# A decoder layer in float32: five products of the last two batches' tails from split operands, and new step orders

## The chip, the cores and the metric

The kernel runs on one core of a Trainium2 chip (trn2). The metric is the time on the device in microseconds (us), the median of several executions; lower is better. The profile is of one execution; its span runs from the first to the last thing recorded on the core.

The engines are TensorE (PE; its weight loads are listed as PEld), VectorE (DVE), ScalarE (ACT), GpSimd (POOL) and SyncE (SP), which only issues transfers here. Each works through its own list of instructions in order, and they meet through semaphores.

## The reference

`x` is 4 batches of 256 tokens by 256 channels, `ctx` the same shape. Cut to what is computed:

```python
x = x + attn(layernorm(x), Wqkv, Wo)         # 16 heads of 16, rope, causal
x = x + xattn(layernorm(x), ctx, mask)       # below
x = x + ffn(layernorm(x), ...)               # 8 experts of 176, best 2, and a shared one of 352

def xattn(h, m, mask):
    scores = einsum('bsd,bmd->bsm', h, m) / sqrt(D)
    scores = where(mask, scores, -1e30)
    return softmax(scores) @ m               # zero for a batch without a valid token
```

All of it is float32, and the results have to be near float32 in accuracy.

## The kernel before

**Steps and orders.** Everything is cut into numbered steps, and a table `ORDER` lists for each engine the order of its steps, written out by hand or by a search outside the kernel. A step of one name on several engines is one piece of work: `s.7` is a product on PE and an exp on ACT. The first number of most steps is the batch; `s` runs over 12 per batch, `m` over 12, `tr` over 8, `qk` over 2, `pv`, `h` over 4.

**Attention of batch b.** `ln1`, `ln1n` (L446), `xt` (transposes, L783; copied by ACT, L434), `qk` and `v` (float32 products, L789), rope on DVE (L639, L642) and POOL (L388), a high part of q and k on ACT (`sh`, L499, L500) and a low part on POOL (L395, L398), which are transposed by `tr` (L938) and copied by ACT and DVE. `m` computes scores (L809, L816) only for the row maxima (DVE, L602); `mt` transposes them (L961), ACT copies them, and SP sends them into q_t by a small transfer (L303), which the first `s` of the batch waits for. `s` computes the scores (L830, L834), ACT takes the exp (L522), casts three of them to a high part (`h`, L529), POOL subtracts to get the low part (`h`, L408), and `pv` (L854) multiplies both with the values. DVE adds up the parts (L665).

**The tail of batch b.** It runs through one bank of PSUM, `ps_tail`. `on` and `ot`: the normalised output is transposed and copied by ACT to `tail_t` (L532); `wo` multiplies it by Wo; DVE adds to the residual (L680). `ln2`, `ln2n`, `t2`: the norm, transposed and copied to `tail_t` (L434). `xs`: times `ctxt_s`, DVE masks and takes the maximum (L691), ACT the exp (L538). `pt`: transposed and copied, scaled by `valid` (L543). `ro`: times `ctx_s`, added on DVE (L701). `ln3`, `ln3n`, `t3`: the norm, transposed, its high part on ACT (L434), its low part on DVE (L709). `lg`, `rk`, `ct`: gate logits, ranks, and the weights of the experts, sent through memory by SP. So a tail has three float32 products, `wo`, `xs` and `ro`, each four products of 128 channels by 256 columns, one after the other at L789. The moments of a norm are taken on DVE (L584), and POOL turns them into scale and shift (L366 to L369).

**The feed-forward part.** 28 times `up` and `dn`, 14 for the first two batches and 14 for the last two. `up.m` multiplies 128 hidden rows by 512 tokens for two weights, from split operands: hi by hi, hi by lo, lo by hi (L776, 12 products of 128x512 in all). ACT applies silu (L562), DVE multiplies (L744) and scales by the experts' weights (L753), ACT casts the high part (`dn`, L568), DVE subtracts for the low part (L758), and `dn.m` adds the product with w3 (L885, 12 products of 128x256). The weights' high parts are cast by ACT (`w12`, `w3`; L468, L477) and their low parts made by POOL (L415, L419), in the place of the raw ones. `up` and `dn` need few engines besides PE and stand between the steps of the last tails.

**Fillers.** `early.n` and `late.n` are n products of zeros (L895) that nobody reads; 16 more run at the start.

The first up step waits for the third norm of batch 1; steps of `up` from 3 on wait for the last exp, since they take over banks; `dn.0` waits for the last rope and values.

## Time and profile before

| | us |
|---|---|
| median of 3 runs | 272.88 (272.65 to 274.71) |
| the profiled execution | 272.15 |
| its span | 270.3 |
| PE busy in the span | 257.3 |
| ACT, DVE, POOL busy | 174.0, 166.3, 119.2 |
| granted clock of PE, mean of the span | 1.00 |

Times in rows are in us unless marked ns. A row of the timeline gives start, duration, engine, line, operation, tiles and count, and in brackets the engine's idle time before it with what ended it. On PE the duration of a product holds a modelled tail that overlaps the next product; the chain of waits shows pieces without it. Counts of the float32 products are twice the calls in the kernel.

### The profile page before, as it was taken

How to read it: one execution, taken by the hardware profiler on the slowest of the kernel's cores; microseconds unless marked ns; L12 is line 12 of the kernel's file. 1: busy time of each engine (PE TensorE's matmuls, PEld its weight loads, DVE VectorE, ACT ScalarE, POOL GpSimd, SP SyncE). 2: the span in 40 equal slices, each digit the busy share in tenths (PEclk: the TensorE clock that was granted, in tenths of full speed). 3: DMA queues.
4: the chain of work that ended last, by engine and by line, in shares of the span. 5: the costliest groups of instructions: out<-in, count | busy, mean ns of one | idle time of the engine just before them, and what ended most of it. 6: DMA issues, size and time to landing. Idle time of an engine off the chain costs nothing.

```text
span 270.3 us, 4890 instructions
## 1 busy us (share of the span) xinstructions
PE 257.3 (95%) x1806; PEld 209.2 (77%) x1806; DVE 166.3 (62%) x361; ACT 174.0 (64%) x290; POOL 119.2 (44%) x133
## 2 busy tenths in 40 slices
PE   7799999999999999959999999999999999999994
PEld 2467666777876888847788988888989898888884
DVE  3388984878778758856452678453755634545463
ACT  7478669979878998979789667536555313223230
POOL 4457915895398897967567453051500000000000
PEclk9999999999999999999999999999999999999999
DMA  7891000000000028000019700000000279000002
GB/s 243 326 397 70 0 2 1 4 2 2 2 0 0 5 79 274 2 5 0 4 49 266 192 1 2 1 0 2 0 0 2 79 168 247 16 0 4 0 0 78
DMA packets 11878, 17.08 MB, mean 63 GB/s; under 512 B 1904, under 2 KB 8272, under 8 KB 11856
## 3 DMA queue, kind: packets, MB, share of 16 engines
q1 hardware_dynamic: 11856, 16.78, 20.1%
q8 instruction: 14, 0.23, 0.4%
q14 instruction: 8, 0.07, 0.1%
HBM read 15.63 MB, written 1.08 MB: 62 GB/s over the span
## 4 chain that ended last, share of the span: by engine, by line
PE 84%; DMA 5%; DVE 4%; ACT 3%; SPq 1%; issue 1%; POOL 1%; DVEq 0%; ACTq 0%
PE bank L776 31%; PE bank L885 14%; PE bank L789 12%; PE bank L938 4%; PE bank L830 4%; DMA res<-x 3%; PE bank L816 3%; PE bank L854 3%; PE bank L783 3%; PE bank L834 3%; PE bank L809 3%; DVE negm L602 2%; PE bank L811 1%; PE bank L818 1%; DMA q_t<-negm_t 1%
## 5 line engine op out<-in xcount | busy, mean ns | idle before, releaser
L408 POOL TENSOR_TENSOR prob_lo<-prob,prob_hi 128x1536 f16<-128x1536 f32 x16 | 49.9, 3121 | 17.4 <-ACT prob_hi L529 17.4
L776 PE MATMUL bank<-x_hi,w_hi 128*128 128x512 f32 x112 | 45.5, 407 | 0.0
L776 PE MATMUL bank<-x_hi,w_lo 128*128 128x512 f32 x112 | 44.2, 395 | 0.0
L776 PE MATMUL bank<-x_lo,w_hi 128*128 128x512 f32 x112 | 44.1, 393 | 0.0
L602 DVE TENSOR_REDUCE negm<-bank 128x2 f32<-128x512 f32 (+1 forms) x48 | 31.5, 687 | 7.0 <-PE bank L811 4.0
L758 DVE TENSOR_TENSOR h_lo<-h_c,h_hi 128x512 fp32r<-128x512 f32 x28 | 19.9, 714 | 23.5 <-ACT h_hi L568 23.4
L744 DVE TENSOR_TENSOR h_c<-bank,h_s 128x512 f32<-128x512 f32 x28 | 19.3, 689 | 24.5 <-PE bank L776 19.8
L562 ACT ACTIVATE h_s<-bank 128x512 f32<-128x512 f32 x28 | 16.7, 598 | 26.2 <-PE bank L776 26.1
L885 PE MATMUL bank<-w_hi,h_hi 128*128 128x256 f32 x112 | 32.8, 293 | 0.1
L568 ACT CAST h_hi<-h_c 128x512 fp32r<-128x512 f32 x28 | 17.2, 616 | 23.5 <-DVE h_c L753 14.0
L885 PE MATMUL bank<-w_lo,h_hi 128*128 128x256 f32 x112 | 31.6, 282 | 0.0
L885 PE MATMUL bank<-w_hi,h_lo 128*128 128x256 f32 x112 | 31.6, 282 | 0.0
L522 ACT ACTIVATE prob<-bank 128x512 f32<-128x512 f32 x48 | 27.5, 597 | 4.5 <-PE bank L834 3.6
L830 PE MATMUL bank<-q_t,k_t 113*128 113x512 f32 (+1 forms) x64 | 23.1, 417 | 2.8 <-DMA q_t<-negm_t 2.8
L776 PEld LDWEIGHTS bank<-x_hi,w_lo 128*128 128x128 f32 x112 | 21.0, 188 | 5.0
L529 ACT CAST prob_hi<-prob 128x1536 f16<-128x1536 f32 x16 | 23.6, 1474 | 1.1 <-PE bank L854 1.0
L776 PEld LDWEIGHTS bank<-x_hi,w_hi 128*128 128x128 f32 x112 | 21.1, 189 | 4.0
L776 PEld LDWEIGHTS bank<-x_lo,w_hi 128*128 128x128 f32 x112 | 21.1, 188 | 4.0
L789 PE MATMUL bank<-wqkv_s,xt_s 128*128 128x512 f32 (+1 forms) x64 | 22.5, 489 | 1.3 <-ACT xt_s L434 1.3
L885 PEld LDWEIGHTS bank<-w_hi,h_hi 128*128 128x128 f32 x112 | 21.3, 190 | 0.8 <-DVE h_lo L758 0.3
L885 PEld LDWEIGHTS bank<-w_lo,h_hi 128*128 128x128 f32 x112 | 21.3, 191 | 0.6
L415 POOL TENSOR_TENSOR w_lo<-w_raw,w_hi 128x512 fp32r<-128x512 f32 x14 | 18.0, 1285 | 7.8 <-ACT w_hi L468 7.8
(128 smaller groups left out, 566.1 us busy)
## 6 DMA issues: line engine op xcount, KB each, us to landing
w_raw<-w SPq DMA_DIRECT2D x3, 1792.0 KB, 8.4
comb_b<-comb_dram SPq DMA_DIRECT2D x8, 256.0 KB, 5.2
res<-x SPq DMA_DIRECT2D x4, 256.0 KB, 6.8
ctxt_s<-ctx_t SPq DMA_DIRECT2D x4, 256.0 KB, 7.6
ctx_s<-ctx SPq DMA_DIRECT2D x4, 256.0 KB, 7.1
out<-res SPq DMA_DIRECT2D x8, 128.0 KB, 1.8
comb_b<-comb_dram SPq DMA_DIRECT2D x4, 224.0 KB, 5.1
wqkv_s<-wqkv SPq DMA_DIRECT2D x1, 768.0 KB, 4.6
```

Of the source, the lines that this page charges most:

```text
L408: eng.tensor_tensor(prob_lo[:, b % 2], prob[:, b % 2], prob_hi[:, b % 2], ALU.subtract)\
L415: eng.tensor_tensor(lo, raw, hi.bitcast(F32), ALU.subtract).then_inc(s[w + "_ok"], 1)
L522: act.activation(prob[:, g % 2, i, :], ps_s[b % 2][:], ACT.Exp, scale=DH ** -0.5)\
L529: act.copy(prob_hi[:, b % 2], prob[:, b % 2]).then_inc(s["p_hi"], 1)
L568: act.copy(h_hi[:, m % 2], h_c[:, m % 2]).then_inc(s["hhi_ok"], 1)
L602: dve.tensor_reduce(maxes, bk[:].rearrange("p (r k) -> p r k", r=maxes.shape[-1]), AX.X, ALU.max, negate=True).then_inc(s["sm_max"], 1)
L744: ins = dve.tensor_tensor(h_c[:, m % 2], h2_bank[h_pair(m)][:], h_s[:, m % 2], ALU.mult)
L758: dve.tensor_tensor(h_lo[:, m % 2], h_c[:, m % 2], h_hi[:, m % 2].bitcast(F32), ALU.subtract)\
L776: ins = pe.matmul(dst, a(k), c(k), start=(k == 0 and i == 0), stop=(k == kt - 1 and i == 2))
L789: ins = pe.matmul(dst, lhs(k), rhs(k), start=(k == 0), stop=(k == KC - 1))
L830: pe.matmul(ps_s[n % 2][:, c * w:(c + 1) * w], k_t[0:SHIFT + 1, b % 2, j, k0:k0 + P], q_t[0:SHIFT + 1, b % 2, j, :, k0:S], start=(c == 0), ...
L885: ins = pe.matmul(y_tile(t), a[:, m % 2, tok], c[:, j, :], start=(j == 0 and i == 0 and t % 2 == 0), stop=(j == FT - 1 and i == 2), skip_g ...
```

## The change

`SPLIT` names five of the twelve products of the tails: xs and ro of batch 2, and wo, xs and ro of batch 3. For these the ACT copy of `ps_tail` writes `tail_hi` in the reduced format instead of `tail_t`; a new DVE step `lo` writes `tail_lo`, the copy's remainder; a new step `sd` makes the high part of Wo, ctx_t or ctx on ACT and the low part on POOL, in the place of the raw data; and PE computes hi by hi, hi by lo and lo by hi instead of one float32 product. The new tiles lie partly where attention's tiles are, so `t2.2` and `sd.0` on ACT wait for the last `pv`. The orders of all engines are new. Cut to the code and to the pieces of the orders that are spoken of below:

```diff
...
+SPLIT = (("xs", 2), ("ro", 2), ("wo", 3), ("xs", 3), ("ro", 3))
...
 ORDER = {
     "SP": """
-        ln1.0 mt.0 mt.1 mt.2 ct.0 ro.0 w3.0 mt.3 ct.1 cb.0 ro.1 y.0 ct.2 ct.3 cb.1 y.1
+        ln1.0 mt.0 mt.1 mt.2 ro.0 mt.3 w3.0 ro.1 ct.0 ct.1 cb.0 ct.2 ct.3 cb.1 y.0 y.1
     """,
     "POOL": """
-        ln1.0 ln1.1 qk.0 sh.0 qk.1 qk.2 sh.1 w12.0 ln1.2 ln1.3 qk.3 w12.1 sh.2 tr.7 sh.3 h.0 qk.4 h.1 sh.4 h.2 h.3
-        qk.5 sh.5 w12.2 ln2.0 w12.3 h.4 h.5 qk.6 sh.6 ln3.0 h.6 qk.7 h.7 sh.7 w12.4 w12.5 h.8 ln2.1 w12.6 h.9 h.10
-        w3.0 w3.1 w12.7 ln3.1 h.11 w12.8 w3.2 h.12 h.13 w3.3 w12.9 ln2.2 h.14 w3.4 w3.5 w3.6 h.15 w12.10 w3.7 ln3.2
-        w12.11 w3.8 w3.9 w3.10 ln2.3 w3.11 w12.12 w3.12 w3.13 w12.13 ln3.3
+        ln1.0 ln1.1 qk.0 ln1.2 sh.0 qk.1 qk.2 sh.1 w12.0 tr.7 w12.1 sh.2 qk.3 sh.3 qk.4 h.0 qk.5 h.1 sh.4 sh.5 h.2
+        h.3 ln1.3 w12.2 h.4 ln2.0 h.5 w12.3 qk.6 w12.4 sh.6 ln3.0 h.6 qk.7 h.7 sh.7 w12.5 h.8 ln2.1 w12.6 h.9 w12.7
+        h.10 h.11 ln3.1 h.12 w12.8 h.13 w3.0 w12.9 h.14 ln2.2 h.15 w3.1 sd.0 w3.2 sd.1 w3.3 w3.4 w12.10 ln3.2 w3.5
+        w12.11 sd.2 w3.6 sd.3 w12.12 w3.7 w3.8 w3.9 ln2.3 w3.10 w12.13 sd.4 ln3.3 w3.11 w3.12 w3.13
...
     "ACT": """
-        ln1n.0 xt.0 ln1n.1 w12.0 sh.0 xt.1 w12.1 v.0 vm.0 tr.0 tr.1 sh.1 v.1 w12.2 tr.4 tr.5 ln1n.2 w12.3 w12.4 sh.2
...
-        h.10 w12.8 s.33 xs.1 w3.0 pt.1 w3.1 s.34 w3.2 s.35 w3.3 mt.3 h.11 w3.4 vm.3 s.36 ln3n.1 s.37 s.38 t3.1 s.39
-        s.40 h.12 lg.1 s.41 up.0 h.13 ct.1 dn.0 up.1 ot.2 s.42 s.43 s.44 w12.9 dn.1 s.45 s.46 h.14 ln2n.2 s.47 up.2
...
+        ln1n.0 xt.0 ln1n.1 v.0 sh.0 xt.1 vm.0 ln1n.2 tr.0 tr.1 sh.1 w12.0 sh.2 w12.1 tr.4 tr.5 xt.2 v.1 sh.3 mt.0
+        vm.1 tr.8 tr.9 s.0 tr.12 s.1 s.2 tr.13 h.0 s.3 s.4 sh.4 s.5 h.1 s.6 sh.5 s.7 s.8 s.9 h.2 s.10 w12.2 s.11
...
+        s.33 w12.7 s.34 xs.1 s.35 pt.1 mt.3 h.11 w12.8 vm.3 s.36 s.37 s.38 h.12 ln3n.1 s.39 s.40 t3.1 s.41 s.42 h.13
+        s.43 lg.1 w12.9 s.44 w3.0 up.0 ct.1 h.14 ot.2 up.1 s.45 dn.0 w3.1 s.46 s.47 h.15 w12.10 up.2 w3.2 ln2n.2
+        dn.1 w12.11 w3.3 dn.2 up.3 sd.0 t2.2 up.4 sd.1 xs.2 dn.3 w3.4 pt.2 up.5 w3.5 w3.6 w3.7 sd.2 up.6 dn.4 ln3n.2
+        t3.2 w12.12 dn.5 lg.2 up.7 up.8 w3.8 sd.3 dn.6 ct.2 w3.9 ot.3 up.9 dn.7 w12.13 ln2n.3 w3.10 up.10 w3.11 dn.8
+        t2.3 sd.4 xs.3 dn.9 dn.10 pt.3 up.11 dn.11 up.12 ln3n.3 w3.12 dn.12 w3.13 t3.3 up.13 dn.13 lg.3 up.14 dn.14
...
     "DVE": """
-        ln1.0 ln1.1 qk.0 ln1.2 qk.1 ln1.3 v.0 qk.2 vm.0 kt.2 kt.3 v.1 qk.3 m.0 m.1 kt.6 m.2 kt.7 m.3 m.4 m.5 m.6 m.7
-        m.8 m.9 m.10 m.11 zero.0 zero.1 kt.10 kt.11 vm.1 qk.4 kt.14 kt.15 m.12 m.13 pv.0 m.14 m.15 m.16 m.17 m.18
...
+        ln1.0 ln1.1 zero.0 zero.1 qk.0 ln1.2 v.0 qk.1 vm.0 qk.2 kt.2 kt.3 qk.3 m.0 m.1 kt.6 m.2 kt.7 m.3 m.4 m.5 m.6
+        m.7 m.8 m.9 m.10 m.11 v.1 vm.1 kt.10 kt.11 qk.4 kt.14 ln1.3 kt.15 qk.5 m.12 m.13 m.14 m.15 m.16 m.17 pv.0
...
+        up.2 pv.14 dn.1 up.3 lo.0 dn.2 xs.2 up.4 pv.15 xc.2 dn.3 lo.1 up.5 ro.2 ln3.2 dn.4 up.6 t3.2 on.3 lg.2 dn.5
+        rk.2 up.7 dn.6 lo.2 up.8 wo.3 ln2.3 dn.7 up.9 dn.8 lo.3 up.10 xs.3 dn.9 xc.3 lo.4 dn.10 ro.3 ln3.3 up.11
...
     "PE": """
-        xt.0 qk.0 qk.1 v.0 xt.1 qk.2 tr.0 tr.1 v.1 tr.2 tr.3 qk.3 tr.4 m.0 tr.5 m.1 tr.6 m.2 tr.7 m.3 xt.2
-        early.1 m.4 m.5 m.6 m.7 m.8 m.9 m.10 m.11 early.3 mt.0 tr.8 tr.9 v.2 tr.10 s.0 tr.11 s.1 tr.12 s.2 tr.13
-        qk.4 s.3 s.4 tr.14 early.3 tr.15 s.5 s.6 m.12 m.13 pv.0 s.7 m.14 m.15 s.8 m.16 s.9 m.17 s.10 m.18 m.19
...
-        m.45 pt.1 m.46 m.47 ro.1 mt.3 pv.9 s.36 s.37 pv.10 s.38 late.1 t3.1 s.39 s.40 pv.11 lg.1 s.41 up.0 s.42
-        s.43 ct.1 late.1 up.1 ot.2 pv.12 wo.2 s.44 pv.13 s.45 s.46 dn.0 s.47 up.2 t2.2 up.3 pv.14 xs.2 up.4 pt.2
-        pv.15 dn.1 ro.2 dn.2 up.5 dn.3 t3.2 up.6 lg.2 dn.4 up.7 ct.2 up.8 ot.3 dn.5 wo.3 dn.6 dn.7 up.9 t2.3
-        up.10 xs.3 up.11 pt.3 dn.8 ro.3 dn.9 dn.10 up.12 t3.3 up.13 dn.11 lg.3 dn.12 dn.13 up.14 ct.3 up.15
...
+        xt.0 qk.0 v.0 qk.1 xt.1 qk.2 tr.0 tr.1 v.1 tr.2 tr.3 qk.3 tr.4 m.0 tr.5 m.1 tr.6 m.2 tr.7 xt.2 m.3
+        early.1 m.4 m.5 m.6 m.7 m.8 m.9 m.10 m.11 early.3 mt.0 tr.8 tr.9 qk.4 tr.10 s.0 tr.11 tr.12 s.1 s.2
+        tr.13 tr.14 qk.5 tr.15 s.3 s.4 m.12 s.5 m.13 s.6 m.14 m.15 m.16 s.7 m.17 pv.0 m.18 m.19 s.8 s.9 m.20
+        s.10 m.21 m.22 s.11 m.23 pv.1 mt.1 tr.16 tr.17 early.2 pv.2 s.12 s.13 tr.18 tr.19 s.14 pv.3 tr.20 tr.21
+        v.2 early.1 ot.0 s.15 tr.22 wo.0 s.16 s.17 tr.23 pv.4 xt.3 s.18 m.24 s.19 m.25 m.26 t2.0 m.27 m.28 xs.0
+        m.29 m.30 qk.6 pt.0 m.31 s.20 ro.0 s.21 m.32 m.33 s.22 qk.7 m.34 m.35 s.23 pv.5 mt.2 t3.0 tr.24 tr.25
+        pv.6 lg.0 tr.26 s.24 s.25 tr.27 v.3 tr.28 pv.7 tr.29 ct.0 tr.30 s.26 s.27 tr.31 ot.1 s.28 m.36 wo.1 s.29
+        s.30 m.37 s.31 m.38 pv.8 m.39 m.40 s.32 m.41 s.33 m.42 t2.1 m.43 m.44 xs.1 m.45 s.34 m.46 s.35 pv.9 m.47
+        pt.1 late.1 mt.3 ro.1 pv.10 s.36 s.37 late.1 s.38 s.39 late.1 s.40 pv.11 late.5 t3.1 s.41 s.42 pv.12
+        s.43 lg.1 s.44 up.0 pv.13 ct.1 s.45 s.46 ot.2 up.1 wo.2 s.47 pv.14 dn.0 up.2 up.3 t2.2 pv.15 up.4 xs.2
+        dn.1 dn.2 pt.2 up.5 ro.2 up.6 up.7 t3.2 dn.3 lg.2 dn.4 up.8 ct.2 dn.5 ot.3 dn.6 wo.3 up.9 up.10 t2.3
+        up.11 xs.3 dn.7 dn.8 pt.3 dn.9 ro.3 dn.10 up.12 up.13 t3.3 dn.11 dn.12 lg.3 up.14 dn.13 up.15 ct.3 up.16
...
-        wo_s = sb("wo_s", [P, KC, C])
-        ctx_s = sb("ctx_s", [P, 2, NT, C])
-        ctxt_s = sb("ctxt_s", [P, 2, KC, S])
+        wo_s, wo_lo = raw_and_lo(sb, "wo", [P, KC, C])
+        ctx_s, ctx_lo = raw_and_lo(sb, "ctx", [P, 2, NT, C])
+        ctxt_s, ctxt_lo = raw_and_lo(sb, "ctxt", [P, 2, KC, S])
...
+        tail_hi = sb("tail_hi", [P, KC, S], F32R)
+        tail_lo = sb("tail_lo", [P, KC, S], F32R)
+        wo_hi = sb("wo_hi", [P, KC, C], F32R)
+        ctx_hi = sb("ctx_hi", [P, 2, NT, C], F32R)
+        ctxt_hi = sb("ctxt_hi", [P, 2, KC, S], F32R)
...
+        def side(n):
+
+            name, b = SPLIT[n]
+            if name == "wo":
+                return wo_s[:], wo_hi[:], wo_lo[:]
+            return [v[:, b % 2] for v in ((ctxt_s, ctxt_hi, ctxt_lo) if name == "xs" else (ctx_s, ctx_hi, ctx_lo))]
         def halves(a_hi, a_lo, b_hi, b_lo):
...
                         .then_inc(s["w3_ok"], 1)
+                elif part == "sd":
+                    raw, hi, lo = side(b)
+                    eng.wait_ge(s["side_hi_ok"], b + 1)
+                    if SPLIT[b][0] == "wo":
+                        eng.wait_ge(s["wo_ps"], NT * SPLIT[b][1])
+                    eng.tensor_tensor(lo, raw, hi.bitcast(F32), ALU.subtract).then_inc(s["side_ok"], 1)
                 elif part == "ln2":
...
                     act.wait_ge(s["ot_ps"], b + 1)
-                    act.copy(tail_t[:], halves_of(ps_tail)).then_inc(s["oh_ok"], 1)
+                    act.copy((tail_hi if ("wo", b) in SPLIT else tail_t)[:], halves_of(ps_tail)).then_inc(s["oh_ok"], 1)
                 elif part == "t2":
-                    xn_hi_copy(1, b, tail_t[:])
+                    if b == 2:
+                        act.wait_ge(s["o_ps"], NG * B)
+                    xn_hi_copy(1, b, (tail_hi if ("xs", b) in SPLIT else tail_t)[:])
                 elif part == "xs":
...
                     act.wait_ge(s["valid_ok"], 1)
-                    act.activation(tail_t[:], halves_of(ps_tail), ACT.Identity, scale=valid[:, b:b + 1])\
+                    act.activation((tail_hi if ("ro", b) in SPLIT else tail_t)[:], halves_of(ps_tail), ACT.Identity, scale=valid[:, b:b + 1])\
                         .then_inc(s["xph_ok"], 1)
+                elif part == "sd":
+                    name, m = SPLIT[b]
+                    raw, hi, lo = side(b)
+                    if b == 0:
+                        act.wait_ge(s["o_ps"], NG * B)
+                    if name == "wo":
+                        act.wait_ge(s["wo_in"], 16)
+                    else:
+                        act.wait_ge(s[("ctxt_in" if name == "xs" else "ctx_in") + str(m % 2)], 16 * (m // 2 + 1))
+                    act.copy(hi, raw).then_inc(s["side_hi_ok"], 1)
                 elif part == "t3":
...
                         .then_inc(s["on_ok"], 1)
+                elif part == "lo":
+                    name, m = SPLIT[b]
+                    if name == "wo":
+                        dve.wait_ge(s["oh_ok"], m + 1)
+                        dve.tensor_tensor(tail_lo[:], halves_of(ps_tail), tail_hi[:].bitcast(F32), ALU.subtract)\
+                            .then_inc(s["tail_lo_ok"], 1)
+                    elif name == "xs":
+                        dve.wait_ge(s["xn_hi_ok1"], m + 1)
+                        dve.tensor_tensor(tail_lo[:], halves_of(ps_tail), tail_hi[:].bitcast(F32), ALU.subtract)\
+                            .then_inc(s["tail_lo_ok"], 1)
+                    else:
+                        dve.wait_ge(s["xph_ok"], m + 1)
+                        dve.scalar_tensor_tensor(out=tail_lo[:], in0=halves_of(ps_tail), scalar=valid[:, m:m + 1],
+                                                 in1=tail_hi[:].bitcast(F32), op0=ALU.mult, op1=ALU.subtract)\
+                            .then_inc(s["tail_lo_ok"], 1)
                 elif part == "wo":
...
                     whole_product(dst, lambda k: a[:, k, tok], lambda k: w[:, k, :]).then_inc(s[name], 1)
+            def split_rows(n, name):
+
+                raw, hi, lo = side(n)
+                pe.wait_ge(s["side_ok"], n + 1)
+                pe.wait_ge(s["tail_lo_ok"], n + 1)
+                for t, dst in enumerate(out_tiles):
+                    tok = slice(t * P, (t + 1) * P)
+                    split_product(dst, lambda k: tail_hi[:, k, tok], lambda k: tail_lo[:, k, tok],
+                                  lambda k: hi[:, k, :], lambda k: lo[:, k, :]).then_inc(s[name], 1)
+
             def row_maxima_scores(b, f):
...
                     pe.wait_ge(s["wo_in"], 16)
-                    product(tail_t, wo_s, "wo_ps")
+                    if ("wo", b) in SPLIT:
+                        split_rows(SPLIT.index(("wo", b)), "wo_ps")
+                    else:
+                        product(tail_t, wo_s, "wo_ps")
                 elif part == "xs":
...
                     pe.wait_ge(s[f"ctxt_in{b % 2}"], 16 * (b // 2 + 1))
-                    product(tail_t, ctxt_s[:, b % 2], "xs_ps")
+                    if ("xs", b) in SPLIT:
+                        split_rows(SPLIT.index(("xs", b)), "xs_ps")
+                    else:
+                        product(tail_t, ctxt_s[:, b % 2], "xs_ps")
                 elif part == "ro":
...
                     pe.wait_ge(s[f"ctx_in{b % 2}"], 16 * (b // 2 + 1))
-                    product(tail_t, ctx_s[:, b % 2], "ro_ps")
+                    if ("ro", b) in SPLIT:
+                        split_rows(SPLIT.index(("ro", b)), "ro_ps")
+                    else:
+                        product(tail_t, ctx_s[:, b % 2], "ro_ps")
                 elif part == "lg":
...
```

`out_tiles` are the two halves of `ps_tail`; `split_product` is the helper of `up` (L776).

## Rows read from the trace of the kernel before

**Rows 1.** The page's first part: busy us, share of the span, instructions.
```profile
PE 257.3 (95%) x1806; PEld 209.2 (77%) x1806; DVE 166.3 (62%) x361; ACT 174.0 (64%) x290; POOL 119.2 (44%) x133
```

**Rows 2.** Table by stretches: us, then each engine's busy us (instructions), clock, DMA share, GB/s.
```profile
119.00:262.00 143.00, 142.93 (x937) 123.27 (x937) 77.06 (x167) 76.30 (x128) 37.70 (x39) 1.00 0.19 49
46.00:115.00 69.00, 68.12 (x607) 54.64 (x606) 52.57 (x119) 60.30 (x103) 54.91 (x43) 1.00 0.11 36
```

**Rows 3.** Timeline of PE: start, us, engine, line, operation, count, idle before.
```profile
64.49 0.66 PE L938 MATMUL bank<-ident,stk 128*128 128x128 f32 x4 [0.37 <-POOL stk L398]
...
114.90 0.38 PE L961 MATMUL bank<-ident,negm 128*16 128x128 f32 x2
...
118.72 0.51 PE L830 MATMUL bank<-q_t,k_t 113*128 113x512 f32 x1 [2.83 <-DMA q_t<-negm_t]
...
121.02 0.66 PE L783 MATMUL bank<-ident,tail 128*128 128x128 f32 x4
...
124.92 0.58 PE L776 MATMUL bank<-x_hi,w_hi 128*128 128x512 f32 x1
```

**Rows 4.** Chain of waits, in order of time: start us, us, what (instruction count).
```profile
172.45 1.43 PE bank L885 x12
173.88 1.73 PE bank L789 x8
...
178.47 2.78 PE bank L776 x12
```

**Rows 5.** Groups by line and form: count, busy us, mean ns, idle before.
```profile
L408 POOL TENSOR_TENSOR prob_lo<-prob,prob_hi 128x1536 f16<-128x1536 f32 x16 | 49.9, 3121 | 17.4 <-ACT prob_hi L529 17.4
...
L522 ACT ACTIVATE prob<-bank 128x512 f32<-128x512 f32 x48 | 27.5, 597 | 4.5 <-PE bank L834 3.6 <-POOL prob_lo L408 0.6
L529 ACT CAST prob_hi<-prob 128x1536 f16<-128x1536 f32 x16 | 23.6, 1474 | 1.1 <-PE bank L854 1.0
...
L415 POOL TENSOR_TENSOR w_lo<-w_raw,w_hi 128x512 fp32r<-128x512 f32 x14 | 18.0, 1285 | 7.8 <-ACT w_hi L468 7.8
...
L753 DVE TENSOR_TENSOR h_c<-h_c,comb_b 128x512 f32<-128x512 f32 x22 | 15.8, 717 | 2.6 <-DVE h_c L744 0.5
...
L468 ACT CAST w_hi<-w_raw 128x512 fp32r<-128x512 f32 x14 | 8.5, 613 | 0.8 <-DMA w_raw<-w 0.8
...
L616 DVE MEMSET q_t<- 64x2048 f32 x2 | 3.5, 1765 | 0.9 <-issue 0.9
...
L709 DVE TENSOR_TENSOR x_lo<-bank,x_hi 128x512 fp32r<-128x512 f32 x4 | 2.8, 690 | 2.8 <-ACT x_hi L434 2.8
...
L532 ACT COPY tail_t<-bank 128x512 f32<-128x512 f32 x4 | 2.3, 586 | 2.4 <-PE bank L783 2.4
```

**Rows 6.** Timeline of DVE, then of POOL, near 149 us.
```profile
149.59 1.22 DVE L753 TENSOR_TENSOR h_c<-h_c,comb_b 128x512 f32<-128x512 f32 x1
...
147.12 3.14 POOL L408 TENSOR_TENSOR prob_lo<-prob,prob_hi 128x1536 f16<-128x1536 f32 x1 [0.56 <-ACT prob_hi L529]
```

**Rows 7.** Timeline of DVE in the opening.
```profile
11.14 0.69 DVE L639 TENSOR_TENSOR rope_c<-bank,cos_t 128x512 f32<-128x512 f32 x1 [3.03 <-PE bank L789]
...
14.27 0.75 DVE L584 BATCH_NORM_STATS2 stats<-res 128x6 f32<-128x256 f32 x2 [1.78 <-DMA res<-x]
```

**Rows 8.** Timeline of ACT, then of POOL, in the opening.
```profile
14.95 0.58 ACT L434 COPY xt_s<-bank 128x512 f32<-128x512 f32 x1
...
14.57 0.73 POOL L395 TENSOR_TENSOR stk<-rot,stk 128x256 fp32r<-128x256 f32 x1 [0.73 <-ACT stk L499]
```

**Rows 9.** Timeline of DVE, then of POOL: the third norm of batch 1.
```profile
115.10 0.88 DVE L701 SCALAR_TENSOR_TENSOR res<-bank,xs_rec,res 128x256 f32<-128x256 f32 x2 [0.57 <-PE bank L789]
...
118.50 0.23 POOL L369 TENSOR_SCALAR shift<-shift 128x2 f32<-128x2 f32 x1
```

**Rows 10.** Timeline of SP's queue: the issue of w3's load.
```profile
101.10 0.37 SPq L335 DMA_DIRECT2D w_raw<-w  x1
```

**Rows 11.** The page's DMA issues: count, KB each, median us to landing.
```profile
w_raw<-w SPq DMA_DIRECT2D x3, 1792.0 KB, 8.4
```

More of the change, by code:

```diff
@@ L68 @@
-        h.10 w12.8 s.33 xs.1 w3.0 pt.1 w3.1 s.34 w3.2 s.35 w3.3 mt.3 h.11 w3.4 vm.3 s.36 ln3n.1 s.37 s.38 t3.1 s.39
-        s.40 h.12 lg.1 s.41 up.0 h.13 ct.1 dn.0 up.1 ot.2 s.42 s.43 s.44 w12.9 dn.1 s.45 s.46 h.14 ln2n.2 s.47 up.2
-        t2.2 up.3 w3.5 w3.6 w3.7 h.15 xs.2 dn.2 pt.2 dn.3 w12.10 up.4 w12.11 up.5 ln3n.2 dn.4 t3.2 dn.5 up.6 lg.2
-        w12.12 w3.8 w3.9 w3.10 up.7 ct.2 dn.6 up.8 w3.11 ot.3 dn.7 w12.13 ln2n.3 up.9 t2.3 dn.8 up.10 w3.12 xs.3
-        dn.9 pt.3 dn.10 w3.13 up.11 ln3n.3 up.12 dn.11 t3.3 up.13 dn.12 dn.13 lg.3 up.14 dn.14 up.15 up.16 dn.15
@@ new lines @@
+        s.18 t2.0 h.5 xs.0 pt.0 s.19 w12.4 s.20 sh.6 h.6 s.21 s.22 w12.5 ln3n.0 s.23 mt.2 t3.0 h.7 tr.24 tr.25 lg.0
+        sh.7 s.24 s.25 w12.6 tr.28 tr.29 ct.0 s.26 ot.1 h.8 s.27 s.28 s.29 v.3 h.9 s.30 s.31 ln2n.1 s.32 t2.1 h.10
+        s.33 w12.7 s.34 xs.1 s.35 pt.1 mt.3 h.11 w12.8 vm.3 s.36 s.37 s.38 h.12 ln3n.1 s.39 s.40 t3.1 s.41 s.42 h.13
+        s.43 lg.1 w12.9 s.44 w3.0 up.0 ct.1 h.14 ot.2 up.1 s.45 dn.0 w3.1 s.46 s.47 h.15 w12.10 up.2 w3.2 ln2n.2
+        dn.1 w12.11 w3.3 dn.2 up.3 sd.0 t2.2 up.4 sd.1 xs.2 dn.3 w3.4 pt.2 up.5 w3.5 w3.6 w3.7 sd.2 up.6 dn.4 ln3n.2
@@ L103 @@
+        dn.14 dn.15 up.17 dn.16 up.18 dn.17 up.19 dn.18 up.20 dn.19 up.21 dn.20 up.22 dn.21 up.23 dn.22 up.24
+        dn.23 up.25 up.26 up.27 dn.24 dn.25 dn.26 dn.27
     """,
```

33 lines of the change are left out of this document (11 added, 22 removed).

## The prediction

> **What bounds the kernel now.** First the page's line of busy shares: TensorE (PE) is busy for 257.3 of 270.3 us [rows 1]. A share hides where, so the table by stretches comes next. From 119 to 262 us PE is busy for 142.93 of 143 us at a granted clock of 1.00 (2.4 GHz), while DVE and ACT are busy for 77 and 76 us; from 46 to 115 us it is 68.12 of 69 us [rows 2]. Then the timeline of PE, for its idle time: the one long wait is 2.83 us, for the small transfer of the row maxima of batch 3, after mt.3 [rows 3]. So the span is nearly the sum of what PE issues, in the order in which it issues it. Anything taken off PE after 119 us comes off the end, as long as the step it is taken from is still ready when PE reaches it. Last, the chain of waits gives the price of a step as PE sees it (start to start, without the modelled tail that the timeline adds): 1.73 us for a float32 product of a tail, 1.43 us for the twelve 128x256 products of a down step, 2.78 us for an up step [rows 4].
>
> **The change part by part.**
>
> 1. Five float32 products become split ones. A split one is 2 tiles x 2 k x 3 = 12 products of 128x128 by 128x256, exactly the shape, type and number of a down step. 1.73 - 1.43 = 0.30 us each, five times: -1.5 us [rows 4]. All five stand where PE never idles [rows 2]. The down step is so near that I take the row as it is; the bounds are 0 (a split product as long as a float32 one) and -1.5.
> By the Trainium skill (FP8 and Floating Point Precision, TensorE Precision Notes) a true float32 product is four passes over the array, and the split leaves the low-by-low one out. By that count alone the saving would be a quarter of 1.73 us, 0.43 each and 2.2 in all; the down step's row says 0.30, and the row decides.
>
> 2. The halves have to be made. Weight side: five ACT casts of 0.61 us and five POOL subtractions of 1.29 us [rows 5], 3.1 and 6.4 us on engines that have room after 119 us. Behind them queue the casts and low halves of w3 and the norms, none of which PE reaches within a microsecond, so I cost them at nothing; if that cover were gone, one subtraction is 1.29 us. Activation side: five DVE subtractions like that of x_lo, 0.69 us [rows 5], each between the ACT copy of ps_tail and the PE product. Between transpose and product the chain was one ACT operation of 0.59 us and is now that plus 0.69, 1.3 to 1.4 with hand-offs. For xs.2, ro.2 and xs.3 the new order puts an up step (2.78) in between: hidden. For wo.3 only dn.6 (1.43) stands there: 0 to 0.1 us of wait. For ro.3 only dn.9, and ACT has the casts dn.9 and dn.10 ahead of pt.3, about 0.6 more: some 0.5 us. I take +0.5, between 0 and 1.5 (all five late by 0.3).
> A DVE operation with two SBUF operands (h_c by comb_b) that ran beside a POOL subtraction took 1.22 us, where 0.72 is the mean [rows 5, 6]. Five more POOL operations make more such meetings, up to 0.5 us each on DVE; they reach PE only through a chain of the kind just named, which is inside the upper bound.
> The Trainium skill (SBUF — State Buffer, SBUF: two separate sides) says that GpSimd and a DVE operation with two SBUF inputs hold one port pair exclusively, for the whole instruction. The row agrees in kind; the page alone would allow 1.29 us a meeting, 6.4 in all, against 2.5 by the row.
>
> 3. The opening. zero.0 and zero.1 (1.77 us each [rows 5]) move from behind m.11 to before qk.0. DVE has 3.0 us free there, up to 11.14 [rows 7], so 3.5 us with their issue overrun by about 1 us, and rot, sh.0 and the ACT copy xt.1 behind it, which began at 14.95 [rows 8], slip by as much. On POOL sh.0 now stands behind ln1.2, whose x is read at 14.27 [rows 7]; sh.0 began at 14.57 [rows 8] and now begins near 16.8, and tr.0 waits for it. Against that, ACT's w12.0 and w12.1 and DVE's ln1.3 and v.1 leave the stretch. Walked step by step with the durations above, mt.0 comes 0.4 us later. Behind mt.0 DVE no longer has the 3.5 us before kt.10, so qk.4 and qk.5 cover the transfer, and the filler products and the wait before tr.15 go: -1.0. Together -0.6 (bounds +1 and -1.5).
>
> 4. mt.3. PE waits 2.83 us from the end of pv.9 to s.36 [rows 3]. Now ro.1 (1.73) is behind mt.3, beside a pv, so that wait falls to about 1.1. It isn't simply won: the third norm of batch 1 starts from ro.1, and up.0 needs it. From ro.1's sum (115.10) through POOL (done 118.73) [rows 9] and ACT to t3.1 at 121.02 [rows 3] took 6 us, and POOL now has h.11 (3.12 [rows 5]) ahead of ln3.1. Walked from mt.3's start: transfer landed at 3.8 us, s.36 to s.38 paced by exps of 0.6, POOL free of h.11 at 5.3, ln3.1 done 6.8, ACT through h.12 and ln3n.1 at 8.8, t3.1 at 8.9, s.41 to s.44 and lg.1 behind exps, up.0 at 13.3. In these 13.3 us stand 9.2 us of products (mt.3, ro.1, three pv, nine s steps, t3.1, lg.1): 4.1 lost. Before, mt.3 to up.0 was 114.90 to 124.92 [rows 3], with 6.3 us of products (three pv, six s steps): 3.7 lost. That is +0.4, less 0.2 for the filler behind ct.1 that goes. The new order itself puts five filler products before t3.1. I take 0 (bounds -2, the transfer's wait won, and +4, rival C).
>
> 5. SP. The load of w3 was issued at 101.10 [rows 10] and lands in 8.4 us [rows 11]; it now goes behind mt.3's transfer, so it lands near 122. ACT reads it first in w3.0, behind s.44, and PE in dn.0, both after 125: nothing, with some 3 us of cover. ct.0 behind ro.1 is waited for by ct.1 alone, and y.0's stores behind cb.1 are not the last: nothing.
>
> 6. The middle, 46 to 115 us, is reordered throughout. Priced by steps its work is about 62 us of 69, so some 6 us are small gaps and fillers. The fillers of the two PE orders are 14 before and 15 after, besides the 16 of the warm-up, so no large stall seems to have gone. One has: sh.4, sh.5 and qk.5 now stand ahead of batch 0's last prob_lo on POOL, and the wait of 0.37 us for stk [rows 3] goes. I take -0.4, between -2 and +2 (the same POOL work delays pv.3, and ot.0 behind it, by up to 2 us).
>
> Sum: -1.5 + 0.5 - 0.6 + 0 + 0 - 0.4 = -2.0 us. The profiled execution took 272.15 us around its span of 270.3, and lies 0.73 below the median of the runs, 272.88. So 268.3 for the span, 270.15 for such an execution, and 270.9 for the median.
>
> **The rivals.**
>
> A. The order gains too: the 1.7 us of the transfer's wait that ro.1 covers stay won, because ACT is ahead of my walk, and the middle loses 1 us less of its 6: 270.9 - 1.7 - 1.0 = 268.2. For it: some 8 us of PE are lost before 125 us, more than item 1 could give. Against it: the number of fillers.
>
> B. The splits' gain is eaten: the five lo chains cost 1.5 us, their upper bound, and the opening's +0.4 stands without the -1.0: 272.88 - 1.5 + 1.5 + 0.4 = 273.3. For it: 0.69 us more in each of five chains. Against it: after 119 us PE waited for no tail before [rows 2].
>
> C. Slower: ACT paces the last attention batch with no up step to cover it. Before, up.0 came after s.41, now after s.44 and pv.12. Three more exps (0.60) and one more prob_hi cast (1.47) lie ahead of it, 3.3 us of ACT, and a prob_lo of 3.12 us on POOL before pv.12 [rows 5]. It decides if ACT comes to s.36 later than 3.8 us after mt.3 (my walk has it there at 3.4), since from there each step of item 4 hangs on an ACT step. Then 3.3 us of ACT, and half of POOL's 3.12 (lg.1 overlaps the rest), come on top for 1.7 us of products bought, and nothing of the opening's gain is left: 272.88 - 1.5 + 0.5 + 3.3 + 1.6 - 1.1 = 275.7.
>
> **How the numbers follow.** The forecast's own case (269.9 to 272.2) has a chance of 0.42, A 0.31, B 0.17, C 0.10. One per cent, about what a measurement of this kernel can tell from no change, is 2.73 us: faster is below 270.15, slower above 275.6. A lies below it but for its upper part, and the lower edge of the forecast's case does too: faster 0.33. C gives 0.09 slower; the rest, 0.58, is within 1%. The range leaves out the lower part of A, and C: 268.0 to 273.8.
>
> **What would show it.** The chain of waits should have pieces of twelve products in 1.43 us for five of the twelve products of the tails. The waits of PE should show no wait for the transfer above 1.5 us, and waits of 0.1 to 0.5 us on tail_lo before wo.3 and ro.3. PE should be busy for all but 1 us from up.0 to the last down steps. up.0 should begin near 126 us, and from there to the end should be about 142.6 us (145.4 before, less 1.5 for the splits and 1.8 for three s steps and a pv already done, plus 0.5). Item 1 is wrong if a split product takes 1.6 us or more; item 2 if PE's waits for tail_lo add up to over 1 us (B); item 4 if up.0 begins before 124 (A) or after 129 (C).

## The result, and the profile after

| us | before | after |
|---|---|---|
| median of 20 runs each, side by side | 272.71 (271.03 to 274.71) | 274.81 (273.08 to 277.95) |
| ratio after to before | | 1.0084, 95% interval 1.0063 to 1.0106 |
| profiled execution, its span | 272.15, 270.3 | 273.39, 271.9 |
| mt.0, up.0 start in it | 34.39, 124.92 | 35.30, 128.85 |
| from up.0 to the end | 145.4 | 143.05 |

The change makes the kernel 0.8% slower; 270.9 was forecast, and 273.8 was the upper end of the range. The mean granted clock of an execution lies between 0.98 and 1.00 for each kernel here, so beside the ratios, which leave out executions over 1.5% above the fastest of their kernel, stand spans "at full clock", the means over the executions at 0.998 or above (44 of 119 of before, mean 269.8; 6 of 20 of after, 271.8). At full clock the change costs 2.0 us.

The page's line for PE and the table by stretches of after (columns as in [rows 1, 2]):
```profile
PE 257.9 (95%) x1822; PEld 208.0 (76%) x1827; DVE 173.6 (64%) x366; ACT 175.8 (65%) x295; POOL 128.7 (47%) x138
...
46.00:115.00 69.00, 67.34 (x622) 53.47 (x624) 51.25 (x115) 59.91 (x103) 53.95 (x44) 1.00 0.03 10
119.00:129.00 10.00, 8.90 (x92) 6.07 (x92) 5.55 (x17) 8.61 (x13) 8.62 (x8) 1.00 0.69 230
129.00:262.00 133.00, 132.57 (x836) 115.59 (x836) 78.66 (x160) 71.99 (x125) 40.63 (x43) 1.00 0.17 49
```
PE's busy time didn't fall at all, though 1.5 us of products went: filler products and the modelled tails count as busy, and hide short waits. PE's idle time moved: 1.66 us in 46 to 115 us, where before had 0.88, and 1.10 in 119 to 129 us, where before had none:
```profile
119.00:129.00 10.00, 10.00 (x99) 7.63 (x98) 5.18 (x19) 9.19 (x14) 7.87 (x4) 1.00 0.00 0
```
That row is before's. ACT is busy there for 9.2 of the 10 us too, more than the 8.6 of after, but PE has up.0 to do from 124.92 on. In after PE has, up to 128.85, only steps that hang on ACT and POOL.

PE's timeline at the steps of [rows 3], then the waits of PE (in total, times, longest):
```profile
115.78 0.39 PE L1018 MATMUL bank<-ident,negm 128*16 128x128 f32 x2 [0.35 <-DVE negm L634]
...
124.01 0.66 PE L830 MATMUL bank<-ident,tail 128*128 128x128 f32 x4 [0.25 <-ACT tail L466]
...
128.85 0.58 PE L823 MATMUL bank<-x_hi,w_hi 128*128 128x512 f32 x1
```
```profile
PE bank L836 <- ACT xt_s L454: 2.4, 2, 1.7
...
PE bank L911 <- POOL prob_lo L422: 0.8, 2, 0.6
...
PE bank L823 <- DVE tail_lo L721: 0.3, 1, 0.3
```
The wait for the transfer, 2.83 us in [rows 3], is gone. mt.3 to up.0 takes 13.07 us (the walk said 13.3). What is left of single waits is small, but for xt_s in the opening: 1.7 us.

To place losses I subtract from a step's start the work that PE issued ahead of it, priced by [rows 4] and like rows (up 2.78, down 1.43, float32 product 1.73, split 1.43, s and m steps 0.36 to 0.44, fillers nothing). Of this "lost time", in before and after: at mt.0 14.6 and 15.5; at mt.1 18.5 and 19.6; at ot.0 20.0 and 22.05; at mt.3 25.8 and 27.8; at up.0 29.9 and 32.1; at up.17 31.3 and 34.1. Three places: the opening (+0.9), mt.1 to ot.0 (+1.0), and the last part, where 1.5 us of products went and 0.5 more is lost than before. With 0.2 at each of two other places that is 2.8 lost and 1.5 gained; 0.3 more behind up.27 makes the 1.6 by which the two spans differ.

### The profile page after: what moved, and what is told of

The parts are those of the page before. It is cut to its first block, busy times and chain, and to the rows that moved or that the text cites. A ratio compares the mean times of both kernels' runs of the same rounds, so it can differ in the third digit from the quotient of the medians.

```text
span 271.9 us, 4950 instructions
## 1 busy us (share of the span) xinstructions
PE 257.9 (95%) x1822; PEld 208.0 (76%) x1827; DVE 173.6 (64%) x366; ACT 175.8 (65%) x295; POOL 128.7 (47%) x138
## 4 chain that ended last, share of the span: by engine, by line
PE 78%; POOL 7%; DVE 5%; issue 3%; ACT 3%; DMA 1%; SPq 1%; DVEq 0%; ACTq 0%; POOLq 0%
PE bank L823 32%; PE bank L942 13%; PE bank L836 8%; PE bank L995 5%; PE bank L887 4%; POOL prob_lo L422 3%; PE bank L911 3%; PE bank L873 3%; PE bank L866 2%; PE bank L891 2%; DVE negm L634 2%; PE bank L830 2%; DMA res<-x 1%; POOL rot L402 1%; PE bank L868 1%
## 5 line engine op out<-in xcount | busy, mean ns | idle before, releaser
L823 PE MATMUL bank<-x_hi,w_hi 128*128 128x512 f32 x112 | 44.9, 401 | 0.0
L634 DVE TENSOR_REDUCE negm<-bank 128x2 f32<-128x512 f32 (+1 forms) x48 | 31.9, 686 | 7.2 <-PE bank L868 4.6
L805 DVE TENSOR_TENSOR h_lo<-h_c,h_hi 128x512 fp32r<-128x512 f32 x28 | 22.7, 812 | 19.7 <-ACT h_hi L600 19.4
L942 PEld LDWEIGHTS bank<-w_hi,h_lo 128*128 128x128 f32 x112 | 21.4, 191 | 0.0
```

The lines of the kernel that those rows point to most:

```text
L634: dve.tensor_reduce(maxes, bk[:].rearrange("p (r k) -> p r k", r=maxes.shape[-1]), AX.X, ALU.max, negate=True).then_inc(s["sm_max"], 1)
L805: dve.tensor_tensor(h_lo[:, m % 2], h_c[:, m % 2], h_hi[:, m % 2].bitcast(F32), ALU.subtract)\
L823: ins = pe.matmul(dst, a(k), c(k), start=(k == 0 and i == 0), stop=(k == kt - 1 and i == 2))
L942: ins = pe.matmul(y_tile(t), a[:, m % 2, tok], c[:, j, :], start=(j == 0 and i == 0 and t % 2 == 0), stop=(j == FT - 1 and i == 2), skip_g ...
```

## The experiments

### Orders and splits apart

Before's orders with the three splits of batch 3, and after's orders without any split:
```diff
-SPLIT = (("xs", 2), ("ro", 2), ("wo", 3), ("xs", 3), ("ro", 3))
+SPLIT = (("wo", 3), ("xs", 3), ("ro", 3))       # and every order of before, with sd, lo put in
+SPLIT = ()                                      # the other: after's orders without sd, lo
```


> The orders of before, with only the three splits of batch 3 (wo, xs, ro) and their sd and lo steps put in by hand. Theory 1 (the splits pay, the new orders cost): each split takes 0.30 us off TensorE (1.43 for 1.73), the chain of a lo step gives back some 0.2 to 0.5 at wo.3 and ro.3, so 0.3 to 0.9 us faster than before, span near 269.7. Theory 2 (the splits themselves cost, through the halves to be made on ACT, POOL and DVE): 0.5 to 2 us slower than before, with waits for tail_lo and for low halves of w3 and h.

> The orders of after without the five splits: the sd and lo steps are left out and all twelve products of the tails are float32. Theory 1: the orders cost 2.8 us before up.0 (TensorE idle summed in the trace: 29.9 us lost before up.0 in before, 32.1 in after, and 0.9 of it before mt.0) and little behind, so 2.0 to 3.0 us slower than before and about 1 us slower than after. Theory 2: the orders are neutral, within 0.5 us of before, and faster than after.


Measured: 1.0006 (0.9975 to 1.0037) for the splits, 270.2 at full clock; 1.0073 (1.0039 to 1.0108) for the orders, 272.2. So at full clock the orders cost 2.4 us, the five splits in them give 0.5 back (by the ratios, 1.0084 with them and 1.0073 without, nothing), and three splits in the old order give nothing. The orders are the fault, and most or all of the splits' gain is eaten.

Table by stretches of the orders alone: from 119 to 129 us PE has the gaps of after, and then, in this execution, its clock is granted at half (1.2 GHz) under up.0, which took 4.1 us (2.97 in after, where the clock stayed at 1.00).
```profile
119.00:129.00 10.00, 8.90 (x89) 6.04 (x90) 5.31 (x16) 8.54 (x13) 8.54 (x8) 0.97 0.70 233
129.00:131.00 2.00, 2.00 (x6) 1.56 (x6) 1.57 (x9) 1.66 (x5) 2.00 (x1) 0.50 0.00 0
```

### The opening

Four tries: after with the memsets back behind m.11 and sh.0 ahead of ln1.2 (e3); every engine in before's order up to mt.0, after's behind it (e5); and, in the order of before, the memsets in front alone (e9), and ln1.2 in front alone (e10). Last, after with sh.0 back alone (e16).
```diff
 "DVE", e9:   -... m.11 zero.0 zero.1 kt.10        +ln1.0 ln1.1 zero.0 zero.1 qk.0
 "POOL", e10: -ln1.1 qk.0 sh.0 qk.1 qk.2 sh.1 w12.0 ln1.2    +ln1.1 qk.0 ln1.2 sh.0 qk.1
 "POOL", e16: -ln1.1 qk.0 ln1.2 sh.0               +ln1.1 qk.0 sh.0 ln1.2
```


> After, with two moves of the opening undone: zero.0 and zero.1 on DVE back behind m.11, and on POOL sh.0 ahead of ln1.2. Theory 1 (the opening is a part of the loss): xt.1's copy on ACT starts near 15 us in place of 16.0, mt.0 near 34.4 in place of 35.3, and the end comes 0.5 to 0.9 us earlier than in after; theory 1b: the idle time of 1.74 us before qk.2 is also what lowers the granted clock to 0.99 in most runs of after, so with it gone the clock of the runs is 1.00 and the median falls by a further 1 us. Theory 2 (the later steps absorb it): mt.0 is earlier but mt.1 (56.7 in after) is not, and the time is that of after within 0.3 us.

> All five splits. Every engine works in the order of before up to its step mt.0 (on DVE up to m.11), and in the order of after behind it; the memsets zero.0 and zero.1 are thus back behind m.11, with v.1 ahead of them. Theory 1 (what the orders lose is lost in three places: 0.9 us before mt.0, 1.0 between mt.1 and ot.0, 0.2 at mt.3 to up.0): mt.0 near 34.5 us in place of 35.3, and the span 0.9 shorter than after's undisturbed one of 271.7, near 270.9, ratio to before near 1.004. Theory 2 (the early memsets paid: with them behind m.11 the copies before tr.10 and tr.14 come later and PE loses before mt.1 what it gained before mt.0): mt.0 near 34.5 but mt.1 not earlier than 56.7, span 271.5 to 272.5, ratio near 1.007.

> The kernel before with one part of the new orders alone: DVE's memsets zero.0 and zero.1 stand ahead of qk.0 and no longer behind m.11. No splits. Theory 1 (the memsets in front push the first rope step on DVE, and rot, the stk copies and tr.0 behind it; that is the opening's loss of 0.9 us): mt.0 starts 0.6 to 1.0 us later than in before (34.4), and what the freed 3.5 us behind m.11 give back before mt.1 is under 0.5: span 0.3 to 0.8 longer. Theory 2 (as the prediction had it: +0.4 before mt.0 and -1.0 behind it): mt.0 near 34.8, mt.1 at 56.8 or earlier, span 0.6 shorter.

> The kernel before with another part alone: POOL's ln1.2 stands ahead of sh.0, as in the new orders, and not behind w12.0. No splits. Theory 1 (POOL waits for the moments of the third x tile before it makes the rows that tr.0 needs, so that tr.0 and all behind it come later): sh.0 on POOL near 16.5 us in place of 14.57, tr.0 and mt.0 later by 0.5 to 1.5 us, span as much longer. Theory 2 (PE has qk.2 to do meanwhile and is not hurt): mt.0 within 0.2 us of before, span the same.

> After with one step moved back: POOL's sh.0 ahead of ln1.2. Theory 1 (PE's tr.0 waits for sh.0, and sh.0 for the third x tile's moments through ln1.2): sh.0 about 15.5 us in place of 16.57, mt.0 0.5 us earlier than 35.4 and the span 0.3 to 0.6 shorter than 271.7. Theory 2 (in the new order the early memsets on DVE alone set the pace): mt.0 and the span within 0.2 of after's.


Measured: e3 1.0211 (mt.0 at 34.82, but v.1 stands behind the memsets there and PE waits 3.0 us for q_t after mt.0; not a clean undo). e5 1.0046 (1.0018 to 1.0073), 271.4 at full clock: mt.0 at 34.79, but mt.1 at 56.99 and not before after's 56.71, as its theory 2 had it. Behind mt.0 PE then waits 0.9 us for DVE's k_t, a wait that after doesn't have, so undoing the opening gives back 0.4 us and not all that it costs. e9 1.0057 (1.0024 to 1.0090). e10 1.0024 (0.9997 to 1.0051), mt.0 at 34.67, 270.6 at full clock. e16 1.0096 (1.0062 to 1.0130), no gain. The profiled execution of e9 took 278.55 us, 4.7 above the median of its twelve, so from it I take how the steps follow on each other, and not a price.

The reason shows when DVE's timelines stand together: second x tile's moments, memsets, first rope step. After, then the memsets alone (e9), then an execution with the memsets where they were (e13, below):
```profile
6.77 0.75 DVE L616 BATCH_NORM_STATS2 stats<-res 128x6 f32<-128x256 f32 x2 [2.03 <-DMA res<-x]
...
10.41 1.76 DVE L648 MEMSET q_t<- 64x2048 f32 x1 [0.48 <-issue]
12.21 0.69 DVE L671 TENSOR_TENSOR rope_c<-bank,cos_t 128x512 f32<-128x512 f32 x1
```
```profile
8.71 0.76 DVE L584 BATCH_NORM_STATS2 stats<-res 128x6 f32<-128x256 f32 x2 [4.09 <-DMA res<-x]
...
12.37 1.76 DVE L616 MEMSET q_t<- 64x2048 f32 x1 [0.48 <-issue]
14.16 0.69 DVE L639 TENSOR_TENSOR rope_c<-bank,cos_t 128x512 f32<-128x512 f32 x1
```
```profile
8.64 0.75 DVE L616 BATCH_NORM_STATS2 stats<-res 128x6 f32<-128x256 f32 x2 [3.95 <-DMA res<-x]
...
11.07 0.69 DVE L671 TENSOR_TENSOR rope_c<-bank,cos_t 128x512 f32<-128x512 f32 x1 [1.39 <-PE bank L836]
```
The moments of the second tile began between 6.7 and 8.7 us, whatever the kernel, as its transfer landed (in twenty profiles, twelve times by 7.1 and four times behind 8.6). With the memsets behind m.11 the rope starts at 10.96 to 11.22 us in all twelve such profiles: the idle time of [rows 7] was slack for the transfer. With the memsets in front it starts 5.45 us after the moments, in all eight: 12.2 at best, 14.2 at worst. PE pays in full (after, then e9):
```profile
16.63 1.98 PE L836 MATMUL bank<-wqkv_s,xt_s 128*128 128x512 f32 x4 [1.74 <-ACT xt_s L454]
```
```profile
18.57 2.48 PE L789 MATMUL bank<-wqkv_s,xt_s 128*128 128x512 f32 x4 [3.80 <-ACT xt_s L434]
```
In e9 the clock is then granted at 0.71 to 0.73 from 19 to 25 us, and mt.0 comes at 38.4. e16, the other late landing with the memsets in front, has mt.0 at 37.9 without a fall of the clock. With the memsets behind m.11 a late landing costs little: mt.0 at 34.8 (e5) and 35.3 (e13), where landings by 7.1 us have 33.8 to 34.7. So the 0.9 us between the two profiled executions of before and after is the price of an early landing.

### The middle

After with sh.5 moved behind h.3 on POOL (e4), on POOL and ACT (e15); before's orders up to ot.0, after's behind (e6); and in the order of before the cluster of qk.5 alone (e17).
```diff
 "PE", e17:   -tr.14 early.3 tr.15 ... m.23 qk.5 mt.1     +tr.14 qk.5 tr.15 ... m.23 mt.1
 "POOL", e17: -qk.4 h.1 sh.4 h.2 h.3 qk.5 sh.5            +qk.4 qk.5 h.1 sh.4 sh.5 h.2 h.3
 "ACT", e17:  -s.7 sh.4 s.8 ... s.13 sh.5                 +sh.4 s.7 sh.5 s.8
```


> After, with sh.5 on POOL moved from before h.2 to behind h.3, so that prob_lo of groups 2 and 3 start 1.5 us earlier. Theory 1 (POOL's order delays pv.3, on.0 and ot.0, which start at 62.4 and 66.0 in after): ot.0 0.8 to 1.5 us earlier, TensorE's lost time before ot.0 down by about as much, unless tr.20 waits for sh.5 instead; 0.3 to 1 us faster than after. Theory 2 (another engine sets that stretch): tr.20 waits as long as pv.3 is earlier, no change within 0.3 us.

> All five splits. Every engine works in the order of before up to ot.0 (DVE up to on.0, ACT up to ot.0, POOL up to sh.5), and in the order of after behind it. Theory 1 (two microseconds of the orders' loss lie before ot.0, and the splits are worth what after showed of them, 0.4 to 1.0): ot.0 near 63.5 us in place of 66.0, less work ahead of it; span 269.5 to 270.2 in an undisturbed execution, ratio to before 0.998 to 1.001. Theory 2 (the loss is a debt of the order as a whole: what is won before ot.0 is lost again before mt.2, since the chain of batch 1 is what paces there): span 271 or more, ratio above 1.004.

> After with sh.5 moved back on both engines that make it: on ACT behind s.13, on POOL behind h.3, as in before. Theory 1 (ACT's casts for sh.5, 1.2 us, and POOL's 1.5 us stand ahead of h.2 and h.3, the low halves that pv.2 and pv.3 wait for; together they make ot.0 late): ot.0 starts 0.8 to 1.2 us earlier than 66.0, and of it 0.5 to 1.0 stays to the end, span 270.7 to 271.2. Theory 2 (ot.0 is late because the row maxima and the exps as a whole come later, and sh.5 is only shifted): ot.0 within 0.3 of 66.0, span 271.7 or more.

> The kernel before with one cluster of the new orders alone: qk.5 on PE behind tr.14, in the place of three filler products, on DVE ahead of m.12, on POOL ahead of h.1, and sh.5 on ACT and POOL ahead of h.2. No splits. Theory 1 (the rope and the rows of qk.5 stand ahead of the row maxima, casts and low halves that batch 0's values wait for; the work is only shifted on PE, the delay of pv.1 to pv.3 is not): ot.0 0.5 to 1.0 us later than in before relative to mt.0 (29.1 us after it), up.0 likewise, span 270.2 to 270.8 against 269.7. Theory 2 (the cluster fills what was filler and wait, and the loss is elsewhere): span 269.7 or less.


Measured: e4 1.0120 (1.0074 to 1.0166), ot.0 at 66.61, no gain: mt.0 to ot.0 takes 31.1 us, in after 30.7. e15 1.0138 (1.0086 to 1.0189), ot.0 at 68.51, worse: 31.9 us from mt.0, which was itself 1.3 late. e6 1.0100 (1.0066 to 1.0135): ot.0 at 63.28, and 2.3 us of wait for ACT's q_t right behind it, where the two orders meet. e17 1.0082 (1.0053 to 1.0112), 272.3 at full clock (three executions): the cluster alone costs 2.5 us. From mt.0 to ot.0 it loses 8.4 us, before 5.4. Of the rest, ot.0 to mt.3 and up.0 to the end repeat before's within 0.1 us. Waits of PE in e17, 34 to 70 us:
```profile
PE bank L853 <- issue: 0.9, 1, 0.9
PE bank L853 <- POOL prob_lo L407: 0.9, 1, 0.9
PE bank L960 <- DVE negm L601: 0.8, 1, 0.8
```
The rope and rows of qk.5 (DVE, ACT and POOL) stand ahead of the maxima and low halves that mt.1 and the values wait for. Undoing one link inside the new order doesn't help, since the other steps were placed for it.

### From mt.3 to up.0

In the order of before: ro.1 behind mt.3 alone (e11); s.42, s.43, pv.12, s.44 ahead of up.0 (e18).
```diff
 "PE", e11: -m.47 ro.1 mt.3 pv.9                          +m.47 mt.3 ro.1 pv.9
 "PE", e18: -s.41 up.0 s.42 s.43 ct.1 late.1 up.1 ot.2 pv.12 wo.2 s.44
            +s.41 s.42 s.43 pv.12 s.44 up.0 ct.1 ot.2 late.1 up.1 wo.2
```


> The kernel before with a third part alone: on PE ro.1 stands behind mt.3 and not ahead of it, so that its 1.73 us lie in the wait for the small transfer of the row maxima. No splits. Theory 1 (the wait becomes shorter but the third norm of batch 1, which starts from ro.1, comes 2 us later and up.0 with it, so nothing is won): mt.3 1.7 us earlier, t3.1 and up.0 at the same time as before within 0.5, span the same within 0.3. Theory 2 (the transfer's wait is real idle time, and its cover is a gain): up.0 1.0 to 1.7 us earlier, span 269 or less.

> The kernel before with the last cluster alone: s.42, s.43, pv.12 and s.44 ahead of up.0 on PE and ACT, and the transposes ot.2 ahead of up.1. No splits. Theory 1 (without an up step between them these steps are paced by ACT's exps of 0.60 us and its casts of 1.47, so PE idles where before it had up.0 to do): up.0 starts 2.5 to 3.5 us later for 1.7 us of products, span 0.8 to 1.5 longer, 270.5 to 271.2; fewer executions at full clock. Theory 2 (nothing is lost, since what ACT has done ahead of up.0 it need not do behind it): span within 0.3 of 269.7.


Measured: e11 1.0050 (1.0018 to 1.0082), 271.0 at full clock, 1.2 more than before. mt.3 is 0.4 us earlier and not 1.7, as theory 1 had it; it waits for the last maxima (PE's timeline of e11):
```profile
114.51 0.39 PE L960 MATMUL bank<-ident,negm 128*16 128x128 f32 x2 [1.32 <-DVE negm L601]
114.73 1.46 PE L788 MATMUL bank<-ctx_s,tail_t 128*128 128x256 f32 x6
```
ro.1 had filled that wait. e18 1.0192 (1.0165 to 1.0219): up.0 at 130.95, and the clock granted at 0.50 to 0.84 from 120 to 136 us. None of its 6 executions was at full clock, but beside them only 1 of before's 11 was. Of its cost, 2.2 us are a wait of pv.12 for DVE's on.2, which is the edit's own; it shows the danger of the place, not the price in after.

### What eats the splits' gain

Before's orders up to pv.15, four splits behind (e7); after with ACT's pt.3 ahead of dn.10 (e8); after with ACT's sd.3, w3.8, w3.9 behind ot.3 (e14); then, from the three splits in before's order, the sums of batch 3 moved to another bank and the wait for tail_lo put off, both at once (e12), and up.10 moved on DVE too (e13).
```diff
 e12: def rows_bank(b): return ps_out if b == 3 else ps_tail     # the sums leave the bank of the transposes
-                pe.wait_ge(s["tail_lo_ok"], n + 1)
                 for t, dst in enumerate(out_tiles(SPLIT[n][1])):
                     for k in range(KC):      # tail_hi by hi, tail_hi by lo
...
+                    if t == 0:
+                        pe.wait_ge(s["tail_lo_ok"], n + 1)
                     for k in range(KC):      # tail_lo by hi
 e13, "DVE": -xs.3 dn.9 lo.2 up.10                        +xs.3 up.10 dn.9 lo.2
```


> Four splits (ro of batch 2; wo, xs and ro of batch 3; the product xs of batch 2 stays float32). Every engine works in the order of before up to pv.15 (DVE dn.2, ACT pt.2, POOL h.15), so the third batch's tail is not touched, and in the order of after behind it, with ACT's copy pt.3 moved ahead of its cast dn.10. Theory 1 (the orders lose before up.0, and the order behind pv.15 is where the splits cost nothing): the start of up.0 as in before, 124.9 us, 4 x 0.30 = 1.2 us less behind it and 0.2 to 0.5 lost on the low halves: span 269.0 to 269.3 undisturbed against 269.9 of before, ratio 0.997. Theory 2 (the low halves and their meetings with POOL eat the gain wherever they stand, as with three splits in the order of before): span 269.9 or more, ratio 1.000 or above.

> After with one step moved: ACT's copy pt.3 (the last tail, from which the low half of ro.3 is made) stands ahead of its cast dn.10 and not behind it. Theory 1 (the wait of 0.3 us for tail_lo before ro.3, and the gap around it, come from the queue of ACT): the wait is gone and the span is 0.3 to 0.5 shorter than after's, 271.2 to 271.4 undisturbed. Theory 2 (the wait is set by PE's own end of dn.9 and the DVE subtraction, not by ACT's queue): no difference beyond 0.1 us.

> After with ACT's casts sd.3, w3.8 and w3.9, and so POOL's subtractions from them, moved behind ACT's copy ot.3. Before, POOL's ran from 172.9 to 176.2 us beside DVE's h_lo for dn.6, which took 1.59 us. Theory 1 (the meeting of the two is what makes h_lo slow and dn.6 and wo.3 late): h_lo takes 0.69 us, the low half tail_lo stands 0.5 to 0.8 us earlier, wo.3 starts 0.5 to 0.8 earlier relative to up.8, span 0.4 to 0.8 shorter than after's 271.7 unless the meeting moves to another operation that PE waits for. Theory 2 (h_lo is slow for another reason): no change of h_lo.

> The three splits of batch 3 in the orders of before, as in the run with three splits, with the cause removed that is suspected of eating their gain: the sums of these three products lie in the bank that the attention has left, not in the bank of the transposes, so that PE may begin with the products of the high half; the wait for tail_lo stands ahead of the first product that reads it, and the four products of a tile with tail_hi go ahead of the two with tail_lo. Theory 1 (the 0.31 us before wo.3 and the 0.47 before ro.3 of that run are the wait for tail_lo at the first product): both gaps vanish, up.0 to up.17 takes 0.6 to 0.8 us less than with three splits, span 269.1 undisturbed against 269.9 of before, ratio 0.997. Theory 2 (the low halves cost DVE and POOL time that comes back elsewhere): the gaps move behind the products and the span stays at 269.9.

> As the run with the late wait for tail_lo, with one more step moved: on DVE up.10 stands ahead of dn.9, where DVE idles, and not behind the low half lo.2, so that the cast and low half of dn.10 no longer come late for PE. Theory 1 (the 0.28 and 0.46 us that PE lost at dn.9 and dn.10 of that run are this queue): both gaps are under 0.1, up.0 to up.17 takes 0.9 us less than in before but for 0.1, span 268.6 to 268.9 undisturbed against 269.7 of before, ratio 0.996. Theory 2 (the gap goes behind the next step again): span 269.2 or more, ratio 0.999.


Measured: e7 1.0142 (1.0111 to 1.0174), 273.8 at full clock, far above theory 1 and above theory 2's bound for another reason than its own: up.0 is where before has it (124.84), and then PE waits 2.0 us for tail_lo and 1.6 for h_lo. The first is, as far as the orders tell, my joint of two orders, the low half queued on DVE behind a step that was late on ACT. The second is a meeting of DVE and POOL as in [rows 6]: a DVE operation with both operands in SBUF beside a POOL subtraction (DVE, then POOL, e7):
```profile
174.23 1.67 DVE L798 TENSOR_TENSOR h_c<-h_c,comb_b 128x512 f32<-128x512 f32 x1 [0.47 <-DVE h_c L789]
175.82 1.75 DVE L803 TENSOR_TENSOR h_lo<-h_c,h_hi 128x512 fp32r<-128x512 f32 x1
```
```profile
174.06 1.29 POOL L438 TENSOR_TENSOR ctxt_lo<-ctxt_raw,ctxt_hi 128x512 fp32r<-128x512 f32 x1 [6.75 <-ACT ctxt_hi L574]
175.31 1.72 POOL L427 TENSOR_TENSOR w_lo<-w_raw,w_hi 128x512 fp32r<-128x512 f32 x1
```
After has one too (DVE, then POOL, then PE at dn.6, which waits for it), and e14 has h_lo back at 0.69 and the meeting one step on (two rows of DVE, then POOL):
```profile
173.41 1.59 DVE L805 TENSOR_TENSOR h_lo<-h_c,h_hi 128x512 fp32r<-128x512 f32 x1
```
```profile
172.93 1.52 POOL L440 TENSOR_TENSOR ctxt_lo<-ctxt_raw,ctxt_hi 128x512 fp32r<-128x512 f32 x1 [5.32 <-ACT ctxt_hi L576]
```
```profile
175.05 0.39 PE L942 MATMUL bank<-w_hi,h_hi 128*128 128x256 f32 x1 [0.17 <-DVE h_lo L805]
```
```profile
174.70 0.69 DVE L805 TENSOR_TENSOR h_lo<-h_c,h_hi 128x512 fp32r<-128x512 f32 x1
...
177.84 1.01 DVE L800 TENSOR_TENSOR h_c<-h_c,comb_b 128x512 f32<-128x512 f32 x1
```
```profile
177.01 1.29 POOL L440 TENSOR_TENSOR ctxt_lo<-ctxt_raw,ctxt_hi 128x512 fp32r<-128x512 f32 x1 [6.57 <-ACT ctxt_hi L576]
```
In e14 (1.0066, 1.0035 to 1.0098) the meeting moved to h_c, and up.8 to wo.3 is only 0.2 us shorter; 272.0 at full clock, no gain. e8 (1.0053, 1.0026 to 1.0080): dn.9 to ro.3 takes 1.81 us where it took 1.96, and it is 271.8 at full clock, as after: theory 2, near enough.

e12: 0.9992 (0.9963 to 1.0021), 269.55 at full clock (four executions). The gaps of 0.31 and 0.47 us before wo.3 and ro.3 are gone; 0.28 and 0.46 come at dn.9 and dn.10. e13: 0.9974 (0.9945 to 1.0003), 269.1 at full clock (three executions), and no gap over 0.1 us between up.8 and up.12. From up.0 to the end, in the profiled executions: 145.4 us before, 145.85 with three splits, 145.6 (e12), 144.7 (e13). Three splits worth 0.9 by price now give 0.7 there. Only e12 and e13 have medians below that of before (272.17 against 272.27, 271.75 against 272.31), and both intervals hold 1, so a gain isn't shown by the times.

## Why the prediction was wrong

The steps that failed are 3 and 6, the opening and the middle: together -1.0 us forecast and +2.1 measured, which is 3.1 of the 3.9 us between 270.9 and 274.81. Step 2 adds 0.5, step 4 adds 0.2. With the measured sizes the sum is -1.5 + 1.0 + 1.1 + 0.2 + 1.0 = +1.8, against 2.0 at full clock.

**What bounds the kernel.** Right: PE's issue sets the span, and what comes off behind up.0 comes off the end (e13). The split product's price was right too; wo.3's first product and the first one behind it, on PE's timeline of after, are 1.44 us apart, ro.2's 1.43:
```profile
176.58 0.28 PE L823 MATMUL bank<-wo_hi,tail_hi 128*128 128x256 f32 x1
...
178.02 0.40 PE L823 MATMUL bank<-x_hi,w_hi 128*128 128x512 f32 x1
```

**Step 2, low halves: +0.5 forecast, 1.0 measured** (0.5 of after's last part beyond before, plus 0.5 that the new order alone saves there, by e2 with its slow up.0 left out). The walk had ro.3 right: 0.5 us is lost ahead of it. It had nothing ahead of dn.6, where 0.3 is lost, as DVE's h_lo met POOL's subtraction and took 1.59 us. So the mis-sized term is the meeting of DVE and POOL: I took up to 0.5 us as its price from [rows 6] and put it at nothing in the sum, inside the upper bound alone. In all five meetings shown the DVE operation ends 0.55 us after the POOL one it met. In [rows 6] POOL ended at 150.26 and DVE at 150.81; above, 174.45 and 175.00, 175.35 and 175.90, 177.03 and 177.57, and in e14 178.30 and 178.85. As such an operation takes 0.69 us alone, the price is what is left of POOL's instruction less 0.14, and [rows 6] was a meeting with 0.67 us left. By this the five cost 0.5, 0.9, 1.0, 1.1 and 0.3 us. The Trainium skill (SBUF — State Buffer, SBUF: two separate sides) has the loser block for the whole instruction; the traces agree, and setting it aside for the price of one row was the error. How much of the 1.0 the meetings make stays open: e14, which moved one, won only 0.2 us up to wo.3 and nothing at the end. A DVE operation that reads PSUM was not slowed: tail_lo at 175.53 took 0.69 us beside POOL's 174.41 to 176.15.

**Step 3, the opening: -0.6 forecast, +1.1 measured.** DVE's overrun was right (12.21 against 11.14). Wrong was what followed: PE's mt.0 came 0.9 later, not 0.4, as the 1.74 us wait for xt_s is not caught up. The gain of 1.0 behind mt.0 did not come (+0.2), as qk.5, put in the fillers' place, delays what mt.1 waits for (e17). And I read the idle time of DVE in one execution as free, where it was slack for a transfer that lands up to 1.9 us later in others.

**Step 4, mt.3 to up.0: 0 forecast, +0.2 measured** against the profiled execution. The walk of 13.3 us met 13.07. up.0 came at 128.85 and not near 126 because mt.3, where the walk starts, was late. "Near 126" put it near 112.8: 114.90, less ro.1, plus pv.9, less the 1.0 that steps 3 and 6 were to win (an estimate from [rows 3] and [rows 4]). It started at 115.78, 3.0 later, which is the miss of steps 3 and 6. So up.0 near 129, my test for rival C, said nothing for C: it doesn't tell a slow stretch from a late start. Against other executions in the order of before, which lose 3.4 us here and not 4.1 (the transfer's wait was 1.9 us in them, 2.83 in before's profile), step 4 is +0.9, so some of C's cost may be in it.

**Step 6, the middle: -0.4 forecast, +1.0 measured.** "One small wait goes" was read from one wait; e17 shows that the cluster of qk.5, which removes that wait, costs 2.5 us alone. In after part of it is made good by other moves, which ones stays open: e4, e6 and e15 did not find a single step.

**Steps 1 and 5** held: no wait for w3 is left, and the splits' products cost what was said. **The rivals.** B came nearest: three splits in the old order bring nothing (e1), and in after 1.0 of their 1.5 us is eaten. A was wrong (ro.1 covers nothing that it had not filled before, e11, and the middle loses 1.0 more, not less); C was not it at the price given; e18 shows its mechanism in the order of before, mixed with a wait that the edit itself made.

## What to carry over

An idle stretch ahead of a step that waits for a transfer is slack, not room: before filling it, look at how late the transfer comes in other executions. A low half made on the way costs what the queue of its engine and the meetings with the other engine make of it; let the products that don't need it go first, and keep the other engine's two-operand subtractions away from that stretch. In a finely placed order, an undo of one step inside the new order proves little; one part of the new order put alone into the old one told more.

## Not expected of the hardware

The clock of PE. In some executions the granted clock fell to 0.50 (1.2 GHz) for some microseconds behind a stretch in which PE waited: in e9 after 3.8 us of idle time (0.71 to 0.73 from 19 to 25 us), in e3 after 3.0 us (0.57 from 42 to 46), and in e2 and e5 behind 119 to 129 us, where up.0 then took 4.1 and 4.5 us in place of 2.97. But the wait alone doesn't decide it: e16 idled for 3.7 us at the place of e9's wait and stayed at 1.00, and after passed 119 to 129 us with the same busy shares as e2 and stayed at 1.00. What decides isn't shown here. Nor is it shown how much rarer full clock becomes: 1 of 12 executions of e9 against 16 of before's 35 beside them speaks for it, none of 6 of e18 against 1 of 11 does not. Where the clock does fall, a wait of PE costs more than its length: in e2, 1.1 us more under up.0.
